# A group-norm and masked batch-norm kernel on one Trainium2 core: the next unit's statistics threaded between the last images of a unit, and part of the last unit given to VectorE

## What is computed

```python
def _gn(v, G=32, eps=1e-5):          # 32 groups of 2 channels, statistics per image and group
    ...
    return ((g - m) / jnp.sqrt(s + eps)).reshape(v.shape)

def _L0_conv_ref(x):                 # x is the normalised g here
    x1 = x.sum(axis=1)
    m = x1 != 0                      # mask: locations whose channel sum is not zero
    ...
    mean = sum_c / total             # per channel, over the masked locations of all images
    ...
    inv = 1.0 / jnp.sqrt(var + EPS)
    xn = x * inv[None, :, None, None]
    out = jnp.where(m[:, None, :, :], xn, x)
    ...
x = x + _L0_conv_ref(_gn(x))
```

## Time and profile before

| | |
|---|---|
| median of 3 runs | 1310.18 us (1310.02 to 1311.68) |
| the profiled execution | 1310.43 us |
| its span | 1308.7 us |
| busy in the span: DVE, ACT, PE, POOL | 996.7, 1008.0, 727.7, 607.6 us |
| mean granted TensorE clock | 0.805 of full |
| DMA | 537.50 MB, mean 411 GB/s |

### The profile page before, as it was taken

One profiled execution on the slowest core, in us unless ns is written; L12 is line 12 of the kernel. 1 busy time (PEld: TensorE's weight loads), 2 busy tenths in 40 slices (PEclk: granted clock), 3 DMA queues, 4 the chain that ended last, 5 costly groups with the idle time before them and its releaser, 6 DMA issues.

```text
span 1308.7 us, 9383 instructions
## 1 busy us (share of the span) xinstructions
PE 727.7 (56%) x2370; PEld 208.7 (16%) x2370; DVE 996.7 (76%) x2243; ACT 1008.0 (77%) x930; POOL 607.6 (46%) x172
## 2 busy tenths in 40 slices
PE   0666565565555564555655546655565555665564
PEld 0111111111111111111111111111111111111110
DVE  6888887777786777777777877778777877777864
ACT  0988887787777887777977779777788777887787
POOL 0555554455344454344544345444445444454344
PEclk9988887888778887778877787777788777877778
DMA  9999999999999999999999999999999999999976
GB/s 378 415 421 421 421 421 421 420 421 421 420 421 421 421 421 421 420 420 422 421 420 420 421 421 418 415 421 421 411 413 421 412 417 409 415 405 399 420 323 259
DMA packets 135223, 537.50 MB, mean 411 GB/s; under 512 B 4096, under 2 KB 4096, under 8 KB 135168
## 3 DMA queue, kind: packets, MB, share of 16 engines
q1 hardware_dynamic: 67584, 268.44, 50.6%
q10 hardware_dynamic: 67584, 268.44, 50.0%
HBM read 268.44 MB, written 268.44 MB: 410 GB/s over the span
## 4 chain that ended last, share of the span: by engine, by line
DMA 55%; ACT 29%; DVE 9%; PE 3%; issue 3%; ACTq 1%; SPq 0%; POOLq 0%; POOL 0%; DVEq 0%
DMA out_dram<-slots 35%; DMA slots<-in_x_dram 20%; ACT slots L280 19%; ACT g L274 10%; DVE stats L393 2%; PE small_ps L320 1%; PE small_ps L330 1%; DVE spread L380 1%; PE small_ps L331 1%; DVE dev L450 1%; ACTq L286 1%; DVE col L457 0%; ACT col L297 0%; SPq L205 0%; DVE dev L422 0%
## 5 line engine op out<-in xcount | busy, mean ns | idle before, releaser
L262 POOL TENSOR_SCALAR g<-slots,group_mean,group_rstd 128x1024 f32<-128x1024 f32 x160 | 606.3, 3789 | 689.1 <-DVE group_bias L441 385.0
L393 DVE BATCH_NORM_STATS2 stats<-slots 128x6 f32<-128x512 f32 x1024 | 658.3, 682 | 244.1 <-DMA slots<-in_x_dram 243.0
L280 ACT ACTIVATE slots<-slots,out_bias,out_scale 128x1024 f32<-128x1024 f32 x512 | 613.6, 1228 | 55.0 <-DVE out_bias L461 40.1
L345 PE MATMUL flush<-g,pair_sum 128*64 128x512 f32 x1536 | 502.4, 764 | 231.3 <-ACT g L274 208.6
L274 ACT ACTIVATE g<-slots,group_bias,group_rstd 128x1024 f32<-128x1024 f32 x352 | 428.9, 1227 | 51.9 <-DVE group_bias L441 51.9
L407 DVE TENSOR_TENSOR sums<-flush,sums 128x512 f32<-128x512 f32 x372 | 251.0, 675 | 24.3 <-PE flush L345 24.3
L345 PEld LDWEIGHTS flush<-g,pair_sum 128*64 128x64 f32 x1536 | 107.3, 166 | 576.4 <-ACT g L274 392.7
L345 PE MATMUL stay<-g,pair_sum 128*64 128x512 f32 x512 | 155.2, 688 | 68.3 <-ACT g L274 61.3
L291 ACT ACTIVATE by_image<-by_image,eps 128x16 f32<-128x16 f32 x32 | 9.8, 308 | 174.4 <-DVE by_image L428 174.4
L320 PE MATMUL small_ps<-spread,group_avg 128*128 128x64 f32 x64 | 21.0, 429 | 121.9 <-DVE spread L424 121.9
L345 PEld LDWEIGHTS stay<-g,pair_sum 128*64 128x64 f32 x512 | 30.6, 152 | 201.1 <-ACT g L274 167.3
(11 more groups left out here) (47 smaller groups left out, 171.4 us busy)
## 6 DMA issues: line engine op xcount, KB each, us to landing
slots<-in_x_dram SPq DMA_DIRECT2D x128, 2048.0 KB, 16.5
out_dram<-slots ACTq DMA_DIRECT2D x128, 2048.0 KB, 30.9
```

The costliest lines, as they stand in the source:

```text
L262: pool.tensor_scalar(g[:, n % G_BUFS, :], image_in_ring(u, i), group_mean[:, n:n + 1], group_rstd[:, n:n + 1], ALU.subtract, ALU.mult).the ...
L280: nc.scalar.activation(v, v, ACT.Identity, bias=out_bias[:, u % 2, i:i + 1], scale=out_scale[:, u % 2, i:i + 1]).then_inc(out_ready, 1)
L345: nc.tensor.matmul(bank[k * ROWS:(k + 1) * ROWS, :], pair_sum[:, :], g[:, n % G_BUFS, k * BLK:(k + 1) * BLK], start=first, stop=final).the ...
L393: last = V.bn_stats(stats[:, u % 2, k * BLOCK_STATS:(k + 1) * BLOCK_STATS], source)
```

## The change

- **The next unit's chain moves into the unit before.** TensorE does the products of unit u+1 after images 11, 11, 12 and 13 of unit u. ScalarE takes the two roots of unit u+1 after outputs 12 and 14 of unit u, and so starts a unit with its normalisations.
- **VectorE's order.** In the pauses of the chain it now makes additions of the unit before (images 10, 12, 13 and 14), and no block of the next unit. The other eight additions stand before blocks 8, 12, 16, 20 and 24.
- **The last unit.** VectorE normalises images 1, 4, 7, 10 and 13 (the list in the code has five) and makes outputs 3, 7, 11 and 15. ScalarE is left with 6 normalisations and 12 outputs, where it had 11 and 16. For the 12 flushed images the last addition and the count become one instruction, which compares the bank's negative with `sums`. The flags of the mask stay in a ring slot for the general path, which no longer makes them.

The core of the diff:

```diff
+    LAST = UNITS - 1
+    dve_images = [i for i in act_images if i % 3 == 1]
+    dve_outs = [i for i in range(B) if i % 4 == 3]
...
+    PRODUCTS_AFTER = (11, 11, 12, 13)
+    ROOTS_AFTER = (12, 14)
...
+    ADDS_BEFORE = {8: (0, 1), 12: (2,), 16: (3, 4), 20: (5,), 24: (6, 7)}
+    ADDS_IN_PAUSE = (8, 9, 10, 11)
...
+            group_root(0)
+            channel_root(0)
+            for u in range(UNITS):
+                mine = [i for i in act_images if u < LAST or i not in dve_images]
+                act.wait_ge(rstd_ready, u + 1)
+                for i in range(B + 1):
+                    if i in mine:
                         normalise(u, i)
-                    if (i - 1) % TILE_IMAGES == 0 and i > TILE_IMAGES:
-                        store(u, (i - 1) // TILE_IMAGES - 1)
-                    put_out(u, i - 1)
-                put_out(u, B - 1)
+                    if i and i % TILE_IMAGES == 1 and i > TILE_IMAGES:
+                        store(u, i // TILE_IMAGES - 1)
+                    if i == 1:
+                        act.wait_ge(scale_ready, (u + 1) * 2)
+                    if i and not (u == LAST and i - 1 in dve_outs):
+                        put_out(u, i - 1)
+                    if u < LAST and i - 1 == ROOTS_AFTER[0]:
+                        group_root(u + 1)
+                    if u < LAST and i - 1 == ROOTS_AFTER[1]:
+                        channel_root(u + 1)
                 store(u, UNIT_TILES - 1)
...
+                    for k in range(SMALLS):
+                        if u < LAST and i == PRODUCTS_AFTER[k]:
+                            product(u + 1, k)
...
+                for k in range(UNIT_BLOCKS):
+                    if u:
+                        for m in ADDS_BEFORE.get(k, ()):
+                            add_sums(u - 1, flushed[m])
                     block_stats(u, k)
-                    if u and k >= LAG and k % 2:
-                        add_sums(u - 1, flushed[(k - LAG) // 2])
-                ahead = [0]
 
                 def meanwhile(n):
-                    if u + 1 < UNITS:
-                        for k in range(ahead[0], ahead[0] + n):
-                            block_stats(u + 1, k)
-                    ahead[0] += n
+                    if u:
+                        add_sums(u - 1, flushed[ADDS_IN_PAUSE[n]])
...
+            def normalise(i):
+                n = LAST * B + i
+                wait_for_g_buffer(dve, n)
+                V.tensor_scalar(g[:, n % G_BUFS, :], image_in_ring(LAST, i), group_mean[:, n:n + 1], group_rstd[:, n:n + 1],
+                                ALU.subtract, ALU.mult).then_inc(g_by_dve, 1)
+
+            def put_out(i):
+                wait_for_g(dve, LAST, i)
+                v = image_in_ring(LAST, i)
+                V.tensor_scalar(v, v, out_scale[:, LAST % 2, i:i + 1], out_bias[:, LAST % 2, i:i + 1],
+                                ALU.mult, ALU.add).then_inc(out_by_dve, 1)
+
+            def count(i):
+                dve.wait_ge(g_summed, (LAST * B + i + 1) * BLOCKS)
                 if i in kept:
-                    source = stay[kept.index(i)][:, :]
-                    dve.wait_ge(g_summed, ((UNITS - 1) * B + i + 1) * BLOCKS)
+                    V.tensor_scalar(not_zero[:, i, :], stay[kept.index(i)][:, :], 0.0, 0.0, ALU.not_equal, ALU.add,
+                                    accum_out=n_part[:, i:i + 1]).then_inc(counted, 1)
                 else:
-                    source = sums[:, flushed.index(i), :]
-                    dve.wait_ge(added, (UNITS - 1) * ADDS + flushed.index(i) + 1)
-                if done >= 2:
-                    dve.wait_ge(counted, done - 1)
-                V.tensor_scalar(not_zero[:, done % 2, :], source, 0.0, 0.0, ALU.not_equal, ALU.add,
-                                accum_out=n_part[:, i:i + 1]).then_inc(counted, 1)
-
-            for i in range(B):
-                if i in flushed:
-                    add_sums(UNITS - 1, i)
-                if i:
-                    count(i - 1, i - 1)
-            count(B - 1, B - 1)
-            dve.wait_ge(counted, B)
+                    at = flushed.index(i)
+                    m = LAST * ADDS + at
+                    dve.wait_ge(added, m + 1 - ADDS)
+                    V.scalar_tensor_tensor(out=not_zero[:, i, :], in0=flush[m % FLUSH_BANKS][:, :], scalar=-1.0,
+                                           in1=sums[:, at, :], op0=ALU.mult, op1=ALU.not_equal,
+                                           accum_out=n_part[:, i:i + 1]).then_inc(added, 1)
+
+            dve.wait_ge(stored[NOT_ZERO_TILE % RING], 16 * (NOT_ZERO_TILE // RING + 1))
+            dve.wait_ge(scale_ready, UNITS * 2)
+            for i in range(B + 2):
+                if i in dve_images:
+                    normalise(i)
+                if i - 1 in dve_outs:
+                    put_out(i - 1)
+                if i >= 2:
+                    count(i - 2)
+            dve.wait_ge(counted, len(kept))
+            dve.wait_ge(added, UNITS * ADDS)
```

65 lines of the change are left out of this document (32 added, 33 removed).

## The result

The changed kernel takes 1312.62 us (median of 20 runs, 1310.64 to 1314.01), beside 1310.66 us for the kernel before on the same chip (20 runs). The ratio is 1.0015, with a 95% interval from 1.0008 to 1.0021: 2.0 us slower, where the prediction had 1309.3, a little faster. The time lies inside the predicted range and moves the other way. One execution in this document, of 1989 us among the six of a variant whose other five took 1302.06 to 1304.42, is left out of that variant's ratio.

A forecast was written before the change was run, and what follows sets the result against it. The prediction took the DMA transfers to bound the kernel. It summed -1.4 (middle) and +0.5 (last unit) to -0.9 on 1310.43 us: 1309.5, or 1309.3 for the median, range 1304.5 to 1315.

The forecast's parts named there:

- The bound: Whole span: DMA transfers set the pace, 40.4 us a unit, against 38.4 us for VectorE's round.
- The chain: Products, roots and pause additions of a unit: additions wait for TensorE's images, `out_scale` at T + 14.2 instead of +8.1.
- T: Start of a unit's first product, forecast 4.85 us after its last tile.
- The middle: Units before the last: a more even store flow gives back 0 to 2.7 us, taken as -1.4.
- The last unit: Last tile to last store, ended by GpSimd's five passes: 44.4 us against 43.9, so +0.5.
- the four steps: Last unit, between starts of GpSimd's five passes: each 5.05 us, waiting for the matmuls of the one before.
- T to GpSimd's first pass: Last unit: the pass waits until image 15 of unit 30 is added, T + 14.2 instead of T + 4.0.
- last pass to last store: Last unit's end: 3.8 us for GpSimd's fifth pass, 1.2 for output 14, and 0.1.
- Behind the last store: End of the span: the counts end under the last store, as before; no time put down.
- TensorE at the high clock: Rival: TensorE runs fast through the chain and the flow becomes even, -5.0 us, 1305.2; chance 0.33.
- The shutting out: Rival, last unit: VectorE's nine long passes and GpSimd's five block each other, 5.2 us more, 1314.5; chance 0.14.
- VectorE's round as the bound: Rival, middle: VectorE's round outgrows the transfers, each us beyond costing some 30 us, about 1335 for one; chance 0.06.

The follow-up runs named there:

- experiment 5: Stores moved: kernel before with paired stores, 1308.1 us; with first three stores two images later, 1310.03; unthreaded last unit, seven g buffers there, plus pairs, 1309.36.
- pairs: The kernel before with the stores of units 0 to 30 issued two at a time: 1308.1 us, ratio 0.9984.
- stores late: The kernel before with the first three stores of each of units 0 to 30 issued two images later, one at a time: 1310.03 us, ratio 0.9999.
- the middle alone: The kernel before with units 1 to 30 threaded and the fused counting, unit 31's chain as before, no VectorE share: 1309.31 us, ratio 0.9994.

## Why the prediction was right or wrong

**The bound.** Right. The transfers set the pace in the middle: an engine wait of 243.0 us became one of 40.9 and the units still take 40.5 us. VectorE's round was forecast at 38.4 us and 2.0 below the transfers'; where it does not wait for loads (the ten rounds up to 425 us) it shows as 38.7, and later 1.8 are left.

**The chain.** Right in its mechanism, 0.7 us short: T was forecast 4.85 us behind the last tile and was 4.96; `out_scale` was forecast at T + 14.2 and began at T + 14.5; image 15 was forecast to be added at T + 14.2 and its matmuls ended at T + 14.7, so that GpSimd's first pass started at T + 14.9. The images, put at 1.76 us, took 1.98, 1.97, 1.97 and 1.92 among the products. The low clock was chosen rightly (0.50 in three windows).

**The middle.** -1.4 was forecast. The last tile came 1.46 us earlier in the profile, and the ratios say 1.0 to 1.6. The size is right by luck, for it was the middle of a range of 0 to 2.7 and the reason given for it is wrong. With the longest gap cut from 19 to 15.8 us the later part gained only 0.11 us a unit, 0.9 in all, and the eleven units ahead of it took 0.05 more each; the mean rate up to the last load did not rise. What moved the last tile is that stores come later (experiment 5). A single profile does not carry the 1.46 either: the counting alone, with the middle of before, had its last tile at 1256.05, 1.3 us earlier than the earlier trace rows. Taken together, the eight threaded kernels with single stores have it at 1254.2 to 1256.0, the four others at 1256.1 to 1257.6.

**The last unit.** This is the step that failed: its +0.5 was +3.29 to the last store and +1.0 behind it. Two terms were too small (the four steps, 20.2 for 22.17, and T to GpSimd's first pass, 14.2 for 14.92), and one was put at nothing (what lies behind the last store, 1.0). With them the sum of -0.9 became +2.83, and the sign turned. By the terms of its own sum:

| term | forecast | profile of the change |
|---|---|---|
| last tile to T | 4.85 | 4.96 |
| T to GpSimd's first pass | 14.2 | 14.92 |
| four steps | 20.2 | 22.17 |
| last pass to last store | 5.1 | 5.12 |
| sum | 44.4 | 47.17 |

The mechanism was named: the first pass waits for image 15 of unit 30, and GpSimd's row sets the end. The biggest error is the steps. They were taken as 5.05 each from the one pair of starts in the earlier trace rows; 0.77 us of the excess are longer passes beside VectorE's, 1.2 are longer waits for TensorE, in two steps whose windows show a clock of 0.66. The kernel before had irregular steps too (1276.11 was 8.06 behind 1268.05); one regular pair was a thin base. The low clock in the steps was in the prediction, but as the other end of the range: 47.2 behind the tile. That 47.17 came is in part luck, since it was to come from 23.0 for the steps and 14.2 for the chain, and came from 22.17 and 14.92.

**Behind the last store** nothing was put down, because the counts "end under the last store as before". They do (the last one starts at 1303.79, and the store lands later); yet the span ends 1.0 us later. The counting alone showed the same 8.5 us without threading and without the share, and so did all the others with the new counting (8.2 to 8.8), so it belongs to the new code. In all three kernels with the old counting (before, pairs, stores late) it was 7.5. The section on the hardware says what the trace shows in that place; why it takes 1.0 us more stays open.

**The rivals.** TensorE at the high clock (0.33) did not come about. The shutting out (0.14) was to give steps about 1.3 us longer; they were 0.5 longer, and less than half of this was the passes. The rule of the Trainium skill, "SBUF — State Buffer", section "SBUF: two separate sides", by which one of the two engines is blocked for the other's whole instruction, is not what the rows show. VectorE's L522 of 0.81 us began at 1275.77, 0.03 us after GpSimd's pass; both ran, VectorE's unchanged and GpSimd's 0.6 us longer than its 3.78, although a second of 0.81 and most of one of 1.40 lay beside it too. (That L522 works in a two-port mode is not shown; it takes 0.81 us for 1024 elements, where a count takes 0.68 for 512.) Others of VectorE's passes grew:

```profile
1275.77 0.81 DVE L522 TENSOR_SCALAR g<-slots,group_mean,group_rstd 128x1024 f32<-128x1024 f32 x1
...
1279.25 1.40 DVE L528 TENSOR_SCALAR slots<-slots,out_scale,out_bias 128x1024 f32<-128x1024 f32 x1
...
1295.92 0.81 DVE L528 TENSOR_SCALAR slots<-slots,out_scale,out_bias 128x1024 f32<-128x1024 f32 x1 [2.32 <-POOL g L284]
```

1.40 us beside GpSimd and 0.81 while GpSimd is idle (its pass ended at 1295.89): the two lengthen each other in part, in this trace by less than a microsecond a pass. The estimate of 0.65 to 1.3 for these passes held but for the 1.40. VectorE's round as the bound (0.06) did not come about after 465 us, the wait for loads being what was left; in the first ten rounds it did, at no cost.

**What the sum hid.** The +0.5 was the sum of two large terms of opposite sign, which only the separate runs show: about -2.6 us for VectorE's share and +5.3 for the threading of the last unit. I had both in one row of passes. Had they been costed apart, the question "why thread the last unit at all" would have been on the page: it has no transfers behind it to hide the longer chain, and one pass of GpSimd is pushed out of it.

## What to carry to other kernels

A reordering that pays in a steady loop is to be costed again for its last round. There the link that it delays has no cover, and the engine that did useful work in the pause (here one of five GpSimd passes) can lose its place. Cost the parts of such a change one by one, since a small sum can hold two large terms, and undo the one with the wrong sign. Before a pattern is blamed for a slow stretch, look whether a fast stretch has it too: here the gap between the stores was the same in both. When loads end earlier, count the bytes of both directions up to that point, to tell a higher rate from stores put off. When a slow engine's row ends last, look first at what frees its buffer; four spare buffers in the last unit gave more than any part of the change.

## What the runs showed of the hardware

- An end behind the last store. The kernels with the new counting end 8.2 to 8.8 us behind the issue of their last store, the others 7.5. The DMA rows from 1302 to 1312 of the kernel with the counting alone (last store 1300.19, end of the span 1308.7), by slices of 0.25 us and by queue:

```profile
GB/s 393 426 377 410 393 410 426 377 459 377 426 426 377 442 377 393 393 33 33 0 0 0 0 0 0 0 0 0 0 33 0 0 0 0 0 0 0 0 0 0
...
q14 instruction: 2, 0.02, 0.4%
```

  The store's bytes are through at 1306.6, and the span ends 2.1 us later; in the kernel before it is 1307.6, and 1.1. One more transfer of the instruction queue (q14) follows at 1309.3, which is 0.6 us after the end of the span. In the kernel before q14 has one transfer in this stretch, at 1307.6, and the one ahead of it came before the last store's issue, at 1300.8. So this queue has no transfer more (34 in all, before 35), but one comes later. Whether this has to do with the extra microsecond was not tried.
- In the chain of the last unit the work of one DMA engine of sixteen is left over for about 8 us (share 0.06, 26 GB/s, in the window from 1265 to 1270, and in the earlier trace rows before). The last tile's statistics had begun at 1255.86, so the loads are over and what it moves are stores.
- The first ten units are paced by VectorE's round when threaded: with the middle alone `out_bias` is at 76.27, 114.98 and then up to 425.49 every 38.7 us (once 39.6), with no wait for loads, while before it was every 36.4 at the start (37.85, 74.27, 110.52). By 465 us both are at the same place (464.85 and 464.75). The slower start cost nothing: the queues were full at 421 GB/s in both from the third slice on.
